# Single-source vector steps of a decoder layer rewritten as two-tensor instructions

## What is computed

```
x = layernorm(x + attention(x))          # 16 heads, three branches a1, a2, a3 mixed by a softmax gate
x = layernorm(x + cross_attention(x, ctx))   # 16 heads of 16 channels, keys and values from ctx, a mask
x = layernorm(x + experts(x))            # 8 experts, 2 active by a router, 256 -> 1024 -> 256

gate = softmax((x @ w_gate).mean(axis=1))         # 3 numbers for each batch row
scores = (x @ w_imp)[..., 0]
_, idx = top_k(scores, 64); idx = sort(idx)       # the 64 tokens that branch 2 keeps
softmax in each branch: exp(scale * s - scale * max(s)) / sum
layernorm: (x - mean) / sqrt(var + 1e-5)
```

## Time and profile before

| | us |
|---|---|
| median of 3 runs | 1801.5 (1798.98 to 1803.38) |
| the profiled execution, its own time | 1801.23 |
| its span, first to last instruction | 1799.5 |
| outside the span | 1.7 |
| PE busy | 1726.6 (96%) |
| DVE busy | 1276.6 (71%) |
| POOL busy | 1040.0 (58%) |
| ACT busy | 881.0 (49%) |
| mean granted TensorE clock | 0.991 of full speed |

### The profile page before, as it was taken

The page is one execution under the profiler, slowest core; times in us unless marked ns, Lnnn a source line. Parts: engine busy times, 40 slices in busy tenths (PEclk is TensorE's granted clock), DMA queues, the critical chain, the costliest instruction groups (busy, mean ns, idle before and its releaser), DMA issues. The chain is left out here.

```text
span 1799.5 us, 34079 instructions
## 1 busy us (share of the span) xinstructions
PE 1726.6 (96%) x11512; PEld 1343.4 (75%) x11512; DVE 1276.6 (71%) x4143; ACT 881.0 (49%) x2827; POOL 1040.0 (58%) x1451
## 2 busy tenths in 40 slices
PE   7899999999999999999999879999999999999998
PEld 4576665765765766766766648999899989998997
DVE  4668878878878877788788657866756575657556
ACT  1665856856846937847658653221322132213221
POOL 2454654745645835746656466764766486648553
PEclk9999999999999999999999989999999999999999
DMA  5000000000000000000000102101010101010001
GB/s 175 7 1 8 7 8 7 2 8 7 2 8 7 1 8 7 2 8 7 2 8 2 48 1 71 48 1 43 5 48 1 48 1 48 1 48 1 1 1 48
DMA packets 24670, 33.91 MB, mean 19 GB/s; under 512 B 5104, under 2 KB 20976, under 8 KB 24368
## 3 DMA queue, kind: packets, MB, share of 16 engines
q1 hardware_dynamic: 24496, 31.73, 5.4%
HBM read 29.62 MB, written 2.10 MB: 18 GB/s over the span
## 5 line engine op out<-in xcount | busy, mean ns | idle before, releaser
L1989 POOL TENSOR_TENSOR h_lo<-h_sb,h_hi 128x512 fp32r<-128x512 f32 x256 | 363.4, 1448 | 109.0 <-DVE h_hi L2164 109.0
L2035 ACT ACTIVATE h_sb<-ps_H,b_sb 128x512 f32<-128x512 f32 x256 | 176.7, 690 | 505.0 <-PE ps_H L2203 483.4
L635 POOL TENSOR_TENSOR pr<-pr,rden 128x128 f32<-128x128 f32 (+2 forms) x768 | 308.1, 437 | 115.6 <-DVE rden L1197 115.6
L2164 DVE CAST h_hi<-h_sb 128x512 fp32r<-128x512 f32 x256 | 243.4, 969 | 127.4 <-ACT h_sb L2035 127.3
L840 ACT ACTIVATE pr<-sm,nmx 128x128 f32<-128x128 f32 (+2 forms) x768 | 311.4, 410 | 32.4 <-DVE nmx L1216 32.3
L2203 PE MATMUL ps_Y<-w_hi,h_hi 128*128 128x256 f32 x1024 | 286.5, 280 | 0.0
L2203 PE MATMUL ps_Y<-w_hi,h_lo 128*128 128x256 f32 x1024 | 286.5, 280 | 0.0
L2203 PE MATMUL ps_Y<-w_lo,h_hi 128*128 128x256 f32 x1024 | 286.4, 280 | 0.0
L670 POOL TENSOR_TENSOR pr<-pr,rden 128x256 f32<-128x256 f32 x256 | 152.3, 617 | 177.2 <-DVE rden L1197 176.4
L1208 DVE CUSTOM_DVE_ANT_0 sm<-ps_S,cmask 128x128 f32<-128x128 f32 (+2 forms) x768 | 191.4, 307 | 34.0 <-PE ps_S L1412 19.2
L2203 PE MATMUL ps_H<-x_hi,w_hi 128*128 128x512 f32 x512 | 199.7, 390 | 1.9 <-POOL w_lo L677 1.9
(11 more groups left out here) (246 smaller groups left out, 3377.2 us busy)
## 6 DMA issues: line engine op xcount, KB each, us to landing
w_raw<-in_W SPq DMA_DIRECT2D x16, 1024.0 KB, 6.3
xin<-in_x SPq DMA_DIRECT2D x8, 256.0 KB, 3.4
cin<-in_ctx SPq DMA_DIRECT2D x8, 256.0 KB, 2.6
w_kw<-in_wink SPq DMA_DIRECT2D x2, 768.0 KB, 6.6
w_ks<-in_selk SPq DMA_DIRECT2D x2, 768.0 KB, 9.9
out<-x SPq DMA_DIRECT2D x3, 512.0 KB, 3.4
b_sb<-in_b SPq DMA_DIRECT2D x1, 1024.0 KB, 4.8
w_qd<-in_dq SPq DMA_DIRECT2D x1, 576.0 KB, 4.9
```

What stands on the lines that cost most here:

```text
L635: last = pool.tensor_tensor(p_, p_, rden[:, h % 2, n:n + 1].to_broadcast([P, width]), ALU.mult)
L1989: pool.tensor_tensor(h_lo[:, s % 2, ht, :], h_sb[:, ht % 4, :], h_hi[:, s % 2, ht, :].bitcast(F32), ALU.subtract).then_inc(lo_sb.sem, 1)
L2035: ins = act.activation(h_sb[:, ht % 4, :], pst[plan.bank(f)][:, :], ACT.Relu, bias=b1[:, 2 * i + s // NCH, ht:ht + 1])
L2164: dve.tensor_copy(h_hi[:, s % 2, ht, :], h_sb[:, ht % 4, :]).then_inc(hi_sb.sem, 1)
```

## The change

Every edited instruction stays where it was on its engine, but for the selection, where two become one. `tensor_scalar` takes one tensor and constants or per-partition scalars; `tensor_tensor` takes two tensors; `scalar_tensor_tensor` takes two tensors and a scalar. All operands of the edited steps lie in SBUF.

- `nmx` (lines 1216 and 1326, 128 times each) and `ve` (line 1268, 16 times) read their constant from a tile that POOL fills at the start, three more set-up instructions there.
- The gate product (line 1120, 8 times) reads its factor as a broadcast tensor.
- `normalise` (line 1276, 32 times) becomes a `scalar_tensor_tensor` with the mean as the scalar and `rstd` broadcast over 256 columns as the second tensor.
- The selection counts the scores that are at most the token's own (`below`, itself included) in place of those above it. With 256 tokens, above + level < 64 says the same as level + 192 < below, so one `scalar_tensor_tensor` does lines 1144 and 1146 (8 times).

```diff
-CONSTS = 12
-FRONT_STEPS = 26
+CONSTS = 15
+FRONT_STEPS = 25
...
+        factors = sb("factors", [P, 16])
+        by_att, by_x, ln_eps = factors[:, 0:6], factors[:, 6:6 + NT], factors[:, 8:8 + NT]
...
+            pool.memset(by_att, -ATT_SCALE).then_inc(ch.step(), 1)
+            pool.memset(by_x, -X_SCALE).then_inc(ch.step(), 1)
+            pool.memset(ln_eps, LN_EPS).then_inc(ch.step(), 1)
...
-                    dve.tensor_scalar(cmp1[:, t, :], srow[:, :], scol[:, t:t + 1], 0.0, ALU.is_gt, ALU.add,
-                                      accum_out=above[:, t:t + 1]).then_inc(c.step(), 1)
+                    dve.tensor_scalar(cmp1[:, t, :], srow[:, :], scol[:, t:t + 1], 0.0, ALU.is_le, ALU.add,
+                                      accum_out=below[:, t:t + 1]).then_inc(c.step(), 1)
...
-                dve.tensor_scalar(gate[:, 0:3], gl[:, 3:6], gl[:, 6:7], None, ALU.mult
+                dve.tensor_tensor(gate[:, 0:3], gl[:, 3:6], gl[:, 6:7].to_broadcast([P, 3]), ALU.mult
...
                 dve.wait_ge(c.sem, c.value())
-                dve.tensor_tensor(rank[:, :], above[:, :], level[:, :], ALU.add).then_inc(c.step(), 1)
-                dve.wait_ge(c.sem, c.value())
-                dve.tensor_scalar(sel[:, :], rank[:, :], float(KEEP), None, ALU.is_lt).then_inc(sel_sb.sem, 1)
+                dve.scalar_tensor_tensor(sel[:, :], level[:, :], float(T - KEEP), below[:, :], ALU.add, ALU.is_lt
+                                         ).then_inc(sel_sb.sem, 1)
...
-                dve.tensor_scalar(nmx[:, h % 2, :], mx[:, h % 2, :], -ATT_SCALE, None, ALU.mult
-                                  ).then_inc(score_sb.sem, 1)
+                dve.tensor_tensor(nmx[:, h % 2, :], mx[:, h % 2, :], by_att, ALU.mult).then_inc(score_sb.sem, 1)
...
-                dve.tensor_scalar(ve[:, :], mv[:, :, 1:2].rearrange("p t o -> p (t o)"), LN_EPS, None,
-                                  ALU.add).then_inc(var_sb.sem, 1)
+                dve.tensor_tensor(ve[:, :], mv[:, :, 1:2].rearrange("p t o -> p (t o)"), ln_eps, ALU.add
+                                  ).then_inc(var_sb.sem, 1)
...
-                    last = dve.tensor_scalar(dst, x1[:, t, :], mv[:, t, 0:1], rstd[:, t:t + 1],
-                                             ALU.subtract, ALU.mult)
+                    last = dve.scalar_tensor_tensor(dst, x1[:, t, :], mv[:, t, 0:1],
+                                                    rstd[:, t:t + 1].to_broadcast([P, C]), ALU.subtract, ALU.mult)
...
-                    dve.tensor_scalar(nmx[:, h % 2, 0:NT], mx[:, h % 2, 0:NT], -X_SCALE, None, ALU.mult
+                    dve.tensor_tensor(nmx[:, h % 2, 0:NT], mx[:, h % 2, 0:NT], by_x, ALU.mult
```

More of the change, by code:

```diff
@@ L362, in attention_stage @@
         scol = sb("scol", [P, NT])
-        rank = sb("rank", [P, NT])
-        above, level = sb("above", [P, NT]), sb("level", [P, NT])
+        below, level = sb("below", [P, NT]), sb("level", [P, NT])
         sel = sb("sel", [P, NT])
```

## The result

The changed kernel takes 1803.9 us in the median (1801.9 to 1807.1, 20 runs) where the kernel before takes 1801.1 (20 runs). The ratio is 1.0015 with a 95% interval of 1.0008 to 1.0021, so it is slower by 2.7 us (1.4 to 3.8).

A forecast was written before the change was run, and what follows sets the result against it. PE, 96% busy and standing only some 34 us over eight rows, was taken to bound the part that could move. Terms -1.8 - 1.2 + 0.8 - 0.2 = -2.4 us gave 1799.0 us, range 1790 to 1806.

The forecast's parts named there:

- A two-tensor form waits as well: Edited DVE lines: an instruction with two SBUF tensors still waits out a whole POOL instruction, so the standing stays.
- nmx, -1.8 us: 256 negations on DVE: 28 ns less each, counted at the 63 places where ACT stood for them; bounds 0 and 7.2 us.
- The selection, woven fronts, 0: Seven of eight selections: 1.17 us of DVE saved each, but covered by PE's score product; 0, bounds 0 and 8.4 us.
- The selection, first front, -1.2 us: First selection: nothing covers it, as DVE's rotary products follow the comparison and POOL stands for them; -1.2 us, bounds 0 and -1.3.
- The first layernorm, 0.1 us a row, +0.8 us: Each row's first layernorm: longer normalisations delay PE's transposes, mostly within a 0.27 us gap; +0.8 us, bounds 0 and +2.1.
- The second layernorm, hidden: Each row's second layernorm: its result has no reader within the row, so its longer normalisation was counted as costing nothing.
- The normalisation's price,: 32 normalisations on DVE: from 402 to 469 ns, +67 ns each, bounded at double, 134 ns, behind a POOL instruction.
- Gate and variance, -0.2: 24 small DVE products, 28 ns less each where free; the eight ahead of the first layernorm count, -0.2 us.
- The waits: Rival: the new form slips by POOL and DVE gets back 66 us; half of PE's 34 us gives 1784 us; chance 0.06.
- DVE's time did not count in full: Rival claimed DVE's time counts in full: 12.5 us gained, 1788.7 us, or 1795 for half of it; chance 0.15.
- no race was lost: Rival: an nmx per row in seven rows also stands for POOL's line 614, 1.27 us; +8.9 us, 1807.7; chance 0.10.
- the normalisation in full: Rival: all 32 normalisations count at 134 ns, +4.3 us in place of +0.8, giving 1802.5 us; chance 0.05.

## Why the prediction was wrong

- *A two-tensor form waits as well.* Right. The changed lines stand as long as before, and with a form beside them that does not stand the wait is shown to be one of the operand form, not of the line.
- *nmx, -1.8 us.* Wrong in size. I took the least duration from another line (142 ns); the new lines have at least 165 ns on six numbers, 5 under the old, and 160 on two. The edit alone measures +0.7 (-0.9 to +2.3). Why two tensors of two numbers take 142 ns at line 1144 and 160 at line 1328 is open.
- *The selection, woven fronts, 0.* Right, as the earlier trace rows said: all of it went into DVE's standing.
- *The selection, first front, -1.2 us.* Wrong, and a misreading. The earlier trace rows show the comparison ending at 47.75 and the rotary products beginning there. I took this for a chain. The changed kernel shows:

```profile
46.26 0.31 DVE L1148 SCALAR_TENSOR_TENSOR sel<-level,below 128x2 f32<-128x2 f32 x1
...
47.81 0.69 DVE L1021 TENSOR_TENSOR pr<-ps_S,cs 128x512 f32<-128x512 f32 x1 [1.24 <-PE ps_S L1414]
```

  DVE now stands 1.24 us for PE's product and starts at 47.81 for 47.75. The term was worth 0. Two engines had come to the same point together: the wait for PE did not show while DVE was still in its comparison.
- *The first layernorm, 0.1 us a row, +0.8 us.* Right: 0.7 in the trace. The pair takes 2.89 us for 2.62, and the gap between its end and the transposes falls from 0.27 us to 0.06, which takes up most of it:

```profile
261.63 1.26 POOL L618 TENSOR_TENSOR rot<-pr 128x512 f32<-128x512 f32 x1
261.69 2.89 DVE L1278 SCALAR_TENSOR_TENSOR x<-x,mv,rstd 128x256 f32<-128x256 f32 x2 [0.81 <-POOL rstd L659]
...
262.85 1.45 POOL L624 TENSOR_TENSOR rot<-pr,rt 128x512 f32<-128x512 f32 x1
...
264.64 0.66 PE L1431 MATMUL ps_T<-ident,x 128*128 128x128 f32 x4
```

- *The second layernorm, hidden.* **This is the step that failed.** I took it as hidden because the row itself does not read its result. But its place is in the program of DVE, between the copy of a head's probabilities and the scores of the next, and these are on the path. What it costs passes on whole: 0.26 us in each of seven rows, +1.8 us in the trace, +2.7 (1.3 to 4.3) in the measured time of this edit alone. The last row has no heads behind it.
- *The normalisation's price,* 67 ns where free and up to 134 behind POOL, was near: 479 - 402 = 77 ns between the least, 126 ns in the median and 134 between the greatest, both beside POOL. Of the 32 instructions 28 run beside POOL and became 120 to 137 ns longer; only the last row's four, with 71 to 74 ns, run free. The prediction had this price; what it did not have is that seven of the eight second layernorms pay it on the path.
- *Gate and variance, -0.2.* Not found. The variance step fell from 168 to 160 ns at the least; the gate product fell from 229 to 163 at the least but only from 588 to 578 in the median, since it stands mostly as well. No step of the trace belongs to either.
- *The rivals.* The waits did not go; DVE's time did not count in full (none of the 8.4 us of the woven selections came out); no race was lost with the nmx form alone, and everything but the normalisation measures +1.1 us (-0.5 to +2.7). The fourth, the normalisation in full, is nearest to what happened: of its 4.3 us 2.5 came.
- *How much DVE's waits are worth* was not asked of the change, and the prediction's bound for it, 34 us from PE's standing, held with much room: of 44 us of nmx standing 8 were on the path, of 14 us in the normalisation about 2, and no kernel here gained more than 12.6. What remains open is which of the 8 us fall on which head of the cross-attention.

With the parts as the trace has them, 1.8 + 0.7 and nothing for the others, the sum is +2.5 us; measured were 2.7, so near in part because the other steps of the trace cancel. The second layernorm by itself does not turn the sign: with it put right the prediction's sum would be -0.6 us. The 4.9 us between -2.4 and +2.5 are 1.8 of it, 1.8 of nmx, 1.2 of the first front and 0.2 of gate and variance, less 0.1 of the first layernorm. That the time still fell inside the stated range is owed to its width, and not to the sum.

## What to carry to other kernels

A step whose result nobody needs soon still takes its time from whatever stands behind it on its engine; ask what the next instruction of that engine is before calling a step hidden. When two engines run side by side, look for instructions whose greatest duration is many times their least: they wait without a semaphore, and the price of the wait depends on the form of the instruction, so a form has to be tried for the wait and not for its arithmetic. A step that ends where the next begins is not proof of a chain; a second engine may have arrived at the same moment.

## What the runs showed of the chip

A VectorE tensor_scalar that also writes an accumulator never stood behind GpSimd: 128 cases of 158 to 164 ns on six numbers, 128 of 154 to 158 on two and 32 of 528 to 541 on 256 columns. The same lines without an accumulator take 170 to 614, 168 to 1692 and 402 to 1355 ns, and with two SBUF tensors 165 to 682, 160 to 1696 and 479 to 1489. The Trainium skill says the same on "SBUF — State Buffer" (section "Who interferes with whom"), where the accumulator form is left out of the list of forms that take the shared ports; the trace agrees.

The standing goes both ways. Beside the first layernorm's pair POOL's line 620 took 1.32 us with the old form and 1.45 with the two-tensor form (line 624 above), and beside the second layernorm's pair its six instructions took 2.50 and 2.76 us: POOL's instructions became longer by about as much as DVE's own. Where the normalisation writes an accumulator, the two of POOL's six that overlap it most take 0.61 and 0.29 us, where they take 0.67 and 0.34 before and 0.79 and 0.47 after the change.

The granted TensorE clock has short falls in the attention part that come at other places in other executions. The kernel with everything but the normalisation had two that the kernel before had not, one of them here (windows: the clock is the figure ahead of the last two). In it the score matmuls of 128x256, 381 ns before, took 635, and all later work moved by 1.4 us:

```profile
190.00:200.00 10.00, 9.65 (x66) 6.91 (x65) 6.26 (x29) 4.93 (x17) 5.16 (x8) 0.83 0.00 0
```

The kernel before, same stretch:

```profile
190.00:200.00 10.00, 9.54 (x73) 6.78 (x72) 7.48 (x35) 6.30 (x25) 5.43 (x8) 1.00 0.00 1
```

PE was busy before and through it (9.65 of the 10 us). 1.00 is the level of 2.4 GHz; 0.83 is a mixture of it and of 1.2 GHz within the 10 us. One such fall is half of the effect under study, which is why the steps of 0.26 us were read place by place and not from the end of the trace.
